# A graph network's first message pass: VectorE's one-hot of two edge tiles, as one instruction or as two with a product between them

## The reference

```python
w = silu(edge_scalars @ Wfc1) @ Wfc2                  # 192 weights of an edge
e0, e1 = f0[edge_src], f1[edge_src]                   # features gathered by source node
mid0 = w0 * e0 * sh0
mid1 = w3 * einsum('eum,em->eu', e1, sh1) / sqrt(3)
mid2 = w1[:, :, None] * e0[:, :, None] * sh1[:, None, :]
mid3 = w2[:, :, None] * e1 * sh0[:, :, None]
n_k = segment_sum(mid_k, edge_dst) / cnt              # mean over the edges of a destination node
```

## Time and profile before

| what | value |
|---|---|
| median of 3 runs | 9313.75 us (9310.38 to 9315.42) |
| profiled execution, its own time | 9304.9 us |
| its span, first to last instruction | 9303.1 us |
| DVE busy over the span | 7166.1 us (77%) |
| POOL busy over the span | 6786.3 us (73%) |
| PE busy over the span | 6550.8 us (70%) |
| ACT busy over the span | 4944.6 us (53%) |
| first one-hot of the first message stage | 2233.4 us |
| last one-hot of it | 6109.5 us |

### The profile page before, as it was taken

The page is one execution under the profiler, slowest core; times in us unless marked ns, Lnnn a source line. Parts: engine busy times, 40 slices in busy tenths (PEclk is TensorE's granted clock), DMA queues, the critical chain, the costliest instruction groups (busy, mean ns, idle before and its releaser), DMA issues. The chain is left out here.

```text
span 9303.1 us, 172881 instructions
## 1 busy us (share of the span) xinstructions
PE 6550.8 (70%) x31164; PEld 4418.8 (47%) x31164; DVE 7166.1 (77%) x21133; ACT 4944.6 (53%) x16490; POOL 6786.3 (73%) x6877
## 2 busy tenths in 40 slices
PE   5666566664555555556555555878799999999999
PEld 3333333332222222222222222346588888888888
DVE  7666666655787887878878787854499999999995
ACT  3444444443444444444444444755477777777774
POOL 5777777777777777777777777567777777777770
PEclk7565565556888888888888888999899999999999
DMA  3222222224666666666666666656566666666667
GB/s 105 92 93 92 93 92 92 92 92 152 217 209 213 209 212 212 209 212 208 212 210 208 213 210 212 219 182 198 168 170 169 168 170 170 168 169 168 171 165 229
DMA packets 1190048, 1591.50 MB, mean 171 GB/s; under 512 B 452553, under 2 KB 967369, under 8 KB 1189577
## 3 DMA queue, kind: packets, MB, share of 16 engines
q1 hardware_dynamic: 790264, 838.69, 29.1%
q0 software_dynamic: 328704, 651.74, 24.2%
q10 hardware_dynamic: 70992, 100.14, 3.0%
HBM read 1000.68 MB, written 1051.46 MB: 221 GB/s over the span
## 5 line engine op out<-in xcount | busy, mean ns | idle before, releaser
L1705 PE MATMUL pair<-prod_m,hot_m 128*128 128x160 f32 x14848 | 2244.8, 304 | 154.7 <-DVE prod_m L1914 118.5
L1587 POOL DMA_INDIRECT feat_m<-feat_tab,rows_m x1856 | 1819.3, 980 | 579.4 <-issue 428.5
L1705 PEld LDWEIGHTS pair<-prod_m,hot_m 128*128 128x128 f32 x14848 | 2043.2, 190 | 356.2 <-issue 355.2
L1737 ACT ACTIVATE prod_m<-part_m,rows_m 128x64 f32<-128x64 f32 x5568 | 1432.3, 337 | 1387.6 <-DVE part_m L1934 1184.0
L1725 ACT ACTIVATE hot_m<-hot_m,rows_m 128x128 f32<-128x128 f32 x5568 | 1728.5, 389 | 688.4 <-DVE hot_m L1897 680.2
L1598 POOL DMA_INDIRECT fetched_m<-feat_tab,index_m x1664 | 1696.5, 1020 | 516.2 <-issue 492.7
L718 POOL DMA_INDIRECT sorted_rows<-rows_e,place_e x1664 | 1612.1, 969 | 541.2 <-issue 504.9
L1686 PE MATMUL bank<-prod_m,hot_m 128*128 128x449 f32 x2476 | 1166.9, 597 | 843.6 <-DVE prod_m L1954 426.4
L1615 POOL DMA_INDIRECT sorted_rows<-later_m,place_m x1248 | 1251.2, 1003 | 464.5 <-issue 375.7
L1914 DVE TENSOR_TENSOR prod_m<-rows_m,feat_m 128x192 f32<-128x192 f32 (+2 forms) x4640 | 1284.5, 309 | 0.0
L1686 PEld LDWEIGHTS bank<-prod_m,hot_m 128*128 128x128 f32 x2476 | 446.6, 201 | 1463.1 <-issue 1161.0
(11 more groups left out here) (251 smaller groups left out, 10147.3 us busy)
## 6 DMA issues: line engine op xcount, KB each, us to landing
agg_tab<-acc_m ACTq DMA_DIRECT2D x928, 320.0 KB
rows_m<-sorted_rows SPq DMA_DIRECT2D x928, 229.0 KB
agg_tab<-acc_m ACTq DMA_DIRECT2D x928, 224.5 KB
rows_m<-sorted_rows SPq DMA_DIRECT2D x928, 197.0 KB
feat_m<-feat_sorted SPq DMA_DIRECT2D x928, 160.0 KB
feat_sorted<-fetched_m SPq DMA_DIRECT2D x208, 640.0 KB
turned_m<-in_turned ACTq DMA_DIRECT2D x159, 256.0 KB
agg_s<-agg_tab SPq DMA_DIRECT2D x98, 320.0 KB, 4.0
```

What stands on the lines that cost most here:

```text
L1587: pool.indirect_dma_start(out=feat[s % RING][:, k, :], out_offset=None, in_=g.feat_tab[l.n], in_offset=bass.IndirectOffsetOnAxis(ap=rows[s ...
L1705: mm = pe.matmul(dst, hot[s % l.hot_bufs][:, k, q, :], rhs, start=(k == 0 and q < 2), stop=(k == ST_TILES - 1), skip_group_check=True)
L1737: ins = act.activation(prod[s % prods][:, k, at:at + S0], part[s % 2][:, k, 0:S0], ACT.Copy, scale=rows[s % HELD][:, k, l.sh_at + m:l.sh_a ...
```

## The change

In the first message stage alone, the one instruction over two tiles becomes two `tensor_scalar`, one for each tile, that take both base_node and the key as per-partition scalars. The first stands where the old one stood, the second between the second and the third of the three final products. The third product becomes a function of its own. The instructions that take part in the second message stage stay as they are.

```diff
+            def tile_hot(step, it, s, k):
+                u = it * TURN + s
+                if k == 0:
+                    dve.wait_ge(rows_here[s % HELD], 16 * (use(it, s, HELD) + 1))
+                    if step is None or step >= l.hot_bufs:
+                        dve.wait_ge(sum_ready, u - l.hot_bufs + 1)
+                ins = dve.tensor_scalar(
+                    hot[s % l.hot_bufs][:, k, 0, :], iota, g.base_node[:, bass.ds(u, 1)],
+                    rows[s % HELD][:, k, l.key_at:l.key_at + 1].bitcast(F32), ALU.add, ALU.is_equal)
+                if k == ST_TILES - 1:
+                    ins.then_inc(hot_ready, 1)
+
...
             def other_products(step, it, s):
...
                 if sends:
-                    half = part[s % 2]
                     vectors(0, 0, 0, 3, 1)
                     scalars(32, 96, 1).then_inc(prod_ready, 1)
-                    dve.wait_ge(part_ready, u * 2 + 2)
-                    dve.tensor_tensor(
...
-                        .to_broadcast([P, ST_TILES, 3, 32]), ALU.mult).then_inc(inner_ready, 1)
...
+            def inner_products(step, it, s):
+                u = it * TURN + s
+                out_p, half = prod[s % prods], part[s % 2]
+                dve.wait_ge(part_ready, u * 2 + 2)
+                dve.tensor_tensor(
...
+                    .to_broadcast([P, ST_TILES, 3, 32]), ALU.mult).then_inc(inner_ready, 1)
...
             def step_(step, it, s):
                 if sends:
                     rank(step, it, s)
-                prepare(step, it, s)
+                    prepare(step, it, s)
+                    stage(1, lambda *a: tile_hot(*a, 0))(step, it, s)
+                    stage(2, first_products)(step, it, s)
+                    stage(l.add_lag, add_up)(step, it, s)
+                    stage(2, other_products)(step, it, s)
+                    stage(1, lambda *a: tile_hot(*a, 1))(step, it, s)
+                    stage(2, inner_products)(step, it, s)
+                    return
                 stage(1, one_hots)(step, it, s)
```

More of the change, by code:

```diff
@@ L1949, in other_products @@
                 if sends:
-                    half = part[s % 2]
                     vectors(0, 0, 0, 3, 1)
                     scalars(32, 96, 1).then_inc(prod_ready, 1)
-                    dve.wait_ge(part_ready, u * 2 + 2)
-                    dve.tensor_tensor(
-                        out_p[:, :, l.inner_at:l.inner_at + V0].rearrange("p k (m c) -> p k m c", m=3),
-                        half[:, :, S0:].rearrange("p k (m c) -> p k m c", m=3),
-                        rows[s % HELD][:, :, l.sh_at:l.sh_at + 3].bitcast(F32).rearrange("p k (m o) -> p k m o", o=1)
-                        .to_broadcast([P, ST_TILES, 3, 32]), ALU.mult).then_inc(inner_ready, 1)
                 else:
@@ L1963, in other_products @@
                     vectors(160, p0 + 32, 2, 3, 1).then_inc(prod_ready, 1)
+            def inner_products(step, it, s):
[3 more added lines that the diff above has]
+                dve.tensor_tensor(
+                    out_p[:, :, l.inner_at:l.inner_at + V0].rearrange("p k (m c) -> p k m c", m=3),
+                    half[:, :, S0:].rearrange("p k (m c) -> p k m c", m=3),
+                    rows[s % HELD][:, :, l.sh_at:l.sh_at + 3].bitcast(F32).rearrange("p k (m o) -> p k m o", o=1)
+                    .to_broadcast([P, ST_TILES, 3, 32]), ALU.mult).then_inc(inner_ready, 1)
             def add_up(step, it, s):
```

## The result

The changed kernel takes 9247.97 us (9242.07 to 9252.59, 5 runs) against 9311.73 us of the kernel before (9304.10 to 9315.42, 5 runs): a ratio of 0.9932, 95% interval 0.9920 to 0.9943. That is 64 us less, where 24 less was forecast (9290 us, range 9257 to 9330): the right side, beyond the range. The profiled executions differ less, 9304.9 and 9247.97 us, with spans of 9303.1 and 9246.2 us: 57 us.

A forecast was written before the change was run, and what follows sets the result against it. POOL's back-to-back DMAs were taken to bound the first message stage until 5824 us, then DVE for 108 steps. -47 us in POOL's stretch and +23 in the tail gave -24: 9313.75 to 9290 us, range 9257 to 9330.

The forecast's parts named there:

- POOL sets the pace, DVE has slack.: First message stage until 5824 us: POOL issues a DMA every 1.315 us; DVE has 0.68 us a step of slack.
- POOL is shut out while DVE runs products of two SBUF tensors back to back.: First message stage: POOL's DMA is held through such a run and gets in when another kind of instruction starts.
- Rival 2: Slower: POOL is held by one instruction at a time, so splitting frees nothing; +23 us, 9337 us, chance 0.14.
- Every one of the 133 began 0 to 0.2 us after the start of L1914.: First message stage, 2400 to 5700 us: the 133 DMAs over 1.45 us, each 0.59 us too long, start there.
- A DMA that falls into the start of L1914 is then held until L1907 ends, 0.27 us less.: Final products, run of three split: shorter hold, worth 36 us over the 133 long DMAs.
- If the number falls half of the way to 86, to 110 ... I take 43.: Long DMAs fall from 133 towards chance's 86; 110 would save 44 of 79 us in the window, 43 taken.
- the -47: The 43 us saving scaled from the 3300 us window to POOL's whole 3608 us stretch: -47 us.
- Rival 3: More than forecast: the long holds go altogether, 86 us gained, 9251 us, chance 0.10.
- The tile's price.: One-hot on DVE: 0.325 us a tile from the row of L1418, 0.65 for both, +0.255 us a step.
- Where it lies: Tiles' price covered by DVE's slack until 5824 us, exposed in the 108 steps behind it: +23 us, 5.9 hidden.

The follow-up runs named there:

- old one-hot moved: Kernel before, with the old one-hot instruction whole between the second and third final product, nothing at the step's start: 9262.0 us, ratio 0.9957.
- delay in front: Kernel before, with an added DVE reduction of 64 PSUM columns (0.13 us a step) ahead of the one-hot: 9331.1 us, ratio 1.0030.
- both tiles in front: Changed kernel, but both one-hot tiles at the old instruction's place, the three final products unsplit: 9265.6 us, ratio 0.9964 against the kernel before.
- tile between first two: Changed kernel, but the second tile between the first and second final product: 9454.6 us, ratio 1.0170 against the kernel before.
- iota in SBUF: Changed kernel, but both one-hot tiles read iota from SBUF instead of PSUM: 9425.9 us, ratio 1.0134 against the kernel before.

## Why the prediction was wrong

*POOL sets the pace, DVE has slack.* Right. POOL waits for nobody in either kernel, and DVE's wait for its sends falls from 513 to 309 us; the forecast said about 300.

*POOL is shut out while DVE runs products of two SBUF tensors back to back.* Right. A PSUM tile, a one-column memset and the old one-hot all end the hold; the same tile from SBUF does not. Rival 2, the hold by single instructions, is refuted in its result: cutting the run does free POOL.

*"Every one of the 133 began 0 to 0.2 us after the start of L1914."* Nearly: five began up to 0.03 us before it, in the end of `add_up`, and were held the same way.

*"A DMA that falls into the start of L1914 is then held until L1907 ends, 0.27 us less."* Right in size: in the changed kernel such a DMA is held by 0.43 us at most, against 0.71, and where the old one-hot splits the run the mean hold is 0.28 us instead of 0.54.

*"If the number falls half of the way to 86, to 110 ... I take 43."* **This is the term that failed**, and with it the -47. I took the starts of POOL's DMAs as near to random against DVE's steps, so that their number could only drift to an even share. They are not random. A DMA that was held in the `part` products ends with the hold, and the next one starts 0.62 us after the first final product. From there on POOL starts a DMA every 1.25 us, and where the second one lands depends on how long DVE's step is. In the kernel before this leads straight to the DMA of the earlier trace rows:

```profile
4006.74 0.35 DVE L1914 TENSOR_TENSOR prod_m<-rows_m,feat_m 128x192 f32<-128x192 f32 x1
4007.36 1.03 POOL L1598 DMA_INDIRECT fetched_m<-feat_tab,index_m  x1 [0.30 <-issue]
4008.69 0.95 POOL L1598 DMA_INDIRECT fetched_m<-feat_tab,index_m  x1 [0.30 <-issue]
```

The step from 4006.74 is 3.09 us long, and the second DMA behind the one at 4007.36 is the one at 4009.94, 0.11 us into L1914. 81 of the 133 long DMAs stand second behind such a start. The changed kernel's step is 0.25 us longer, and the tile at the place of the first DMA does not hold it, so the second one comes before the run and not in it:

```profile
4977.61 0.35 DVE L1926 TENSOR_TENSOR prod_m<-rows_m,feat_m 128x192 f32<-128x192 f32 x1
4978.22 0.95 POOL L1598 DMA_INDIRECT fetched_m<-feat_tab,index_m  x1 [0.30 <-issue]
4979.47 0.95 POOL L1598 DMA_INDIRECT fetched_m<-feat_tab,index_m  x1 [0.30 <-issue]
4980.73 0.95 POOL L1598 DMA_INDIRECT fetched_m<-feat_tab,index_m  x1 [0.30 <-issue]
4980.95 0.35 DVE L1926 TENSOR_TENSOR prod_m<-rows_m,feat_m 128x192 f32<-128x192 f32 x1
```

Here is the same for the short steps of each kernel. They are the shortest regular kind, with one long instruction of `rank` in them, 205 to 230 in the window. The table takes those that have a DMA starting 0.55 to 0.72 us after their first final product:

| kernel | length of a short step, us | such steps | second DMA behind: its start against the next first final product, us (median) | its mean above 0.95 us |
|---|---|---|---|---|
| before | 3.09 | 104 | 0.11 after | 0.47 |
| old one-hot moved | 3.09 | 53 | 0.08 after | 0.35 |
| delay in front | 3.22 | 73 | 0.03 before | 0.68 |
| both tiles in front | 3.34 | 67 | 0.13 before | 0.00 |
| changed | 3.34 | 127 | 0.19 before | 0.01 |
| tile between first two | 3.34 | 120 | 0.61 after | 0.39 |
| iota in SBUF | 3.21 | 138 | 0.61 after | 0.33 |

So the hits at the start of the run fell from 126 to 13, far below the even share of 753 x 0.12 / 1.3 = 70, chiefly because the step became longer. This needs no split: both tiles in front, with the same step, has 50. What takes the number on from 50 to 13 was not separated. The last two rows show the loop of the two slow kernels (9455 and 9426 us): the DMA is held at 0.6 us, and the second one behind it is at 0.6 us again. That the change avoids this loop was luck; the prediction did not look for it. In the window POOL's time beyond 0.95 us a DMA fell from 152 to 89 us, by 63 where I took 43, and over the stage that is -67 us instead of -47. Rival 3 named 9251 us, nearly the time that came, but for another reason: it let the long holds go with the place where the run stops, and they went with the length of the step.

*The tile's price.* The row of L1418 led to the right price: 404 ns, and 0.32 us from start to start where 0.325 was forecast. The rule of the Trainium skill (VectorE: DVE Perf Modes, the section on the TRN2 errata), 0.258 us, did not. *Where it lies:* the tail took 9 us more, not 23. 109 steps x (2 x 0.32 - 0.39) = 27 us were added, as said, and a step more than before, 3 us. But more of it was hidden: the waits for ACT's root and for features fell from 29 to 9 us, where I had credited 6.

The two errors add up, 20 us and 14 us in the same direction, and that is the distance from 24 to 58 us. The rest, to the 64 us between the medians, is within what runs of one kernel differ by.

What stays open: why a hit is held for only the first product (0.18 us) when a memset stands behind the second, and for both (0.28 us and more) when a longer instruction does. Also open is how the other 52 long DMAs of the kernel before came about.

## What to carry to other kernels

Where GpSimd's indirect DMAs set the pace, look at the maximum of their durations beside the median, and at what DVE runs when a long one starts. Runs of DVE instructions with two SBUF inputs are what to break up, and the cheapest break found here is a memset of one column, 0.01 us a step for 0.8% of the kernel. Two engines that hold each other do not meet at random: count where the starts fall before pricing them by an average, and follow the DMAs behind a hold, one every 1.25 us here, into the next step with its new length. Distrust a small shift that wins or loses by rhythm alone (here +0.13 us a step cost 21 us, +0.245 gained 37, and one tile put 0.2 us earlier cost 207).

## What the runs showed of the hardware that was not expected

- A memset of 128x1, 59 ns long, put ahead of a product of two SBUF tensors delays that product by 0.01 us only; in the timeline it even starts 0.02 us after the product. Yet it cuts POOL's hold from 0.54 to 0.18 us.
- A second per-partition scalar has a price on DVE. In the kernel before a `tensor_scalar` with one of them, from PSUM, takes 308 ns for 96 elements, and the next starts 0.225 us after it. 32 elements more would make that 0.26 us, an estimate from L1914 and L1907 (0.07 us for 64). The tile with two such scalars and 128 elements takes 404 ns and 0.32 us from start to start.

```profile
L898 DVE TENSOR_SCALAR feat_e<-pair,scale_e x98: 301/308/310, 84.1 to 2051.8; 128x96 f32<-128x96 f32 x98
```

- A `tensor_scalar` of 128x128 fp32 from SBUF takes 342 ns and holds POOL; from PSUM it takes 404 ns and does not. The shorter one made the kernel 178 us slower.
- DVE doing 0.13 us more in each step made one kernel 134 us faster.
